# One edge pass over a graph, items of one destination block: destination rows by a one-hot product instead of a gather

## The reference, cut to what matters

```python
h = relu(layernorm(x))
x_i, x_j = h[src], h[dst]                       # 64 features each
out_i = softplus(concat([x_i, edge_attr], -1) @ W).reshape(-1, 4, 64)
out_j = softplus(concat([x_j, edge_attr], -1) @ W).reshape(-1, 4, 64)
alpha = softplus((concat([out_i, out_j], -1) * att).sum(-1))
alpha = softplus(batchnorm(alpha))
alpha = segment_softmax(alpha, src, N)
x = x + segment_sum(out_j * alpha[:, :, None], src, N).mean(1) + bias
```

## Time and profile before

| | us |
|---|---|
| median of 3 runs | 15,799.41 (15,780.74 to 15,803.04) |
| the profiled execution | 15,805.04 |
| its span, first to last instruction | 15,803.4 |
| POOL busy | 10,427.8 (66%) |
| DVE busy | 7,340.1 (46%) |
| PE busy | 7,014.0 (44%) |
| ACT busy | 4,611.6 (29%) |

### The profile page before, as it was taken

One profiled execution on the slowest core, in us unless ns is written; L12 is line 12 of the kernel. 1 busy time (PEld: TensorE's weight loads), 2 busy tenths in 40 slices (PEclk: granted clock), 3 DMA queues, 4 the chain that ended last, 5 costly groups with the idle time before them and its releaser, 6 DMA issues. The chain is left out here.

```text
span 15803.4 us, 144151 instructions
## 1 busy us (share of the span) xinstructions
PE 7014.0 (44%) x27704; PEld 5113.7 (32%) x27704; DVE 7340.1 (46%) x13765; ACT 4611.6 (29%) x8149; POOL 10427.8 (66%) x9774
## 2 busy tenths in 40 slices
PE   2344444444444444420255408953333553333377
PEld 1233333333333333310255402333333333333233
DVE  9566666666666666657377600122222222222301
ACT  5455555555555455521366500000000000000000
POOL 7677777777777777747777770057777447777500
PEclk9777777777766677655566659755555555555578
DMA  0444444444444444490366507521111221111155
GB/s 14 111 129 128 128 129 129 130 129 129 133 129 129 129 129 129 129 78 8 98 183 181 157 5 253 203 62 26 26 26 26 56 77 25 26 26 26 19 191 212
DMA packets 867765, 1601.13 MB, mean 101 GB/s; under 512 B 510485, under 2 KB 518653, under 8 KB 817264
## 3 DMA queue, kind: packets, MB, share of 16 engines
q1 hardware_dynamic: 536176, 1173.07, 24.4%
q0 software_dynamic: 331392, 426.19, 11.6%
HBM read 1091.51 MB, written 505.30 MB: 101 GB/s over the span
## 5 line engine op out<-in xcount | busy, mean ns | idle before, releaser
L1401 POOL DMA_INDIRECT l2s_got<-rel_d,l2s_idx x3232 | 3223.3, 997 | 2141.6 <-POOLq L1398 1244.2
L1427 PE MATMUL l2s_ps<-l2s_got,l2s_oh 128*128 128x65 f32 (+1 forms) x6464 | 1473.3, 421 | 2770.4 <-PEq L1425 2763.5
L1427 PEld LDWEIGHTS l2s_ps<-l2s_got,l2s_oh 128*128 128x128 f32 x6464 | 1409.0, 330 | 2837.5 <-issue 2837.5
L1120 POOL DMA_INDIRECT count_d<-all_list_val,all_list_idx x1568 | 1810.2, 1154 | 503.4 <-issue 463.2
L647 POOL DMA_INDIRECT edge_gath<-h_d,edge_idx_d x1576 | 1682.0, 1067 | 480.3 <-issue 480.3
L643 POOL DMA_INDIRECT edge_gath<-h_d,edge_idx_s x1576 | 1665.0, 1056 | 480.2 <-issue 390.6
L1102 DVE TENSOR_TENSOR net_acc<-net_acc,l2s_ps 128x65 f32 (+1 forms) x3232 | 720.4, 223 | 2705.5 <-DVEq L1449 1813.1
L655 POOL DMA_INDIRECT rows_d<-edge_rows,edge_place x1576 | 1652.7, 1049 | 480.5 <-issue 479.7
L790 DVE SCALAR_TENSOR_TENSOR edge_rows<-edge_z,edge_soft 128x1024 f32<-128x1024 f32 x784 | 952.6, 1215 | 2011.2 <-DVEq L788 2010.9
L723 PE MATMUL edge_z<-edge_w_i,edge_in_i 128*128 128x256 f32 x3140 | 1346.3, 519 | 761.6 <-PEq L752 448.7
L716 PE MATMUL edge_tp<-all_ident,edge_gath 128*128 128x128 f32 x1576 | 428.1, 427 | 1932.5 <-DMA edge_gath<-h_d,edge_idx_d 1649.1
(11 more groups left out here) (342 smaller groups left out, 12493.9 us busy)
## 6 DMA issues: line engine op xcount, KB each, us to landing
at_rows<-rows_d SPq DMA_DIRECT2D x444, 528.0 KB
count_d<-edge_zero SPq DMA_DIRECT2D x196, 1024.0 KB
edge_srow<-in_src SPq DMA_DIRECT2D x197, 512.0 KB, 5.1
edge_lrow<-lo_d SPq DMA_DIRECT2D x197, 512.0 KB, 6.0
l1s_cnt<-count_d SPq DMA_DIRECT2D x49, 1600.0 KB, 6.6
l3s_cnt<-count_d SPq DMA_DIRECT2D x49, 1600.0 KB, 7.0
rel_d<-l2t_out SPq DMA_DIRECT2D x100, 768.0 KB, 3.2
l1s_cnt<-count_d SPq DMA_DIRECT2D x49, 1536.0 KB, 6.7
```

The lines of the kernel that those rows point to most:

```text
L1120: pool.indirect_dma_start(out=cells, out_offset=bass.IndirectOffsetOnAxis(ap=net.list_idx[i][:, k:k + 1], axis=0), in_=net.list_val[i][:, ...
L1401: pool.indirect_dma_start(out=got[r][:, j, 0:cols], out_offset=None, in_=table, in_offset=bass.IndirectOffsetOnAxis(ap=idx[i][:, k:k + 1], ...
L1427: ins = pe.matmul(ps[q][:, j, 0:wide], oh[q][:, j, :], got[r][:, j, 0:wide], start=True, stop=True)
```

## The change

It does these things, all for the edge pass:

- The pass no longer runs over the 1,568 tiles but over the items by destination, 1,616 with padding: 101 trips of two groups. An item has all its valid destinations in one block of 128 nodes. Edges of a tile that belong to the other item go to spare rows.
- The gather of h by dst goes. Per item SP loads the block's 128 rows of h (`nodes`) by a plain DMA, and PE multiplies them with a one-hot of the local destination (`oh_dstT`, from the broadcast row `drow`), which gives the features on partitions at once.
- Edge features are loaded per item, by two DMAs of 64 x 128, since an item's tile is known only at run time (`item`, read into registers).
- The source half is multiplied with W as the stationary side: `z_i` has output features on partitions, 512 edges in a product. Its att dots are 16 products of two columns on PE (`dots`); only the destination half keeps the multiply and reduce on DVE.
- z_i and z_j have one buffer each. The bf16 id rows are half as large; srow is f32.
- The item lists move from `edge_softmax` into a new stage `dst_items` ahead of the edge pass, with a further list of source rows. The 50 counting passes become one comparison of the first destination of each tile (`lead`) with the block bounds.
- `gsrc`, the second list of sources, is gone. The zeros are written in two pieces a group.

```diff
-            def load_group(c0, q):
-                e0 = c0 * P
-                sp.wait_ge(ea_free, 1).then_inc(ea_free, -1)
-                sp.dma_start(in_i[q][D:2 * D, :], a["edge_t"][:, bass.ds(e0, GP)]).then_inc(ea_loaded[q], 16)
-                sp.dma_start(in_j[q][0:D, :], a["edge_t"][:, bass.ds(e0, GP)]).then_inc(ea_loaded[q], 16)
+            def load_group(w0, q):
+                sp.wait_ge(item_listed, 1).then_inc(item_listed, -1)
+                tiles = item_values(nc, sp, item[q][0:1, :, 0], T - 1)
+                blocks = item_values(nc, sp, item[q][0:1, :, 1], NU)
+                sp.wait_ge(feats_free, 1).then_inc(feats_free, -1)
+                for j in range(G):
+                    with Scratch(nc, sp):
+                        sp.dma_start(nodes[q][:, j, :], net.h0_d[bass.ds(blocks[j], P), :]).then_inc(nodes_loaded[q], 16)
+                        for n in TWO:
+                            sp.dma_start(feats[q][D:2 * D, n, j * P:(j + 1) * P],
+                                         edge_tiles[:, bass.ds(tiles[j], 1), :].rearrange("d n e -> d (n e)")
+                                         ).then_inc(feats_loaded[q], 16)
...
                 sp.wait_ge(ids_free, 1).then_inc(ids_free, -1)
+                for row, flat in ((drow, net.loc_d), (lrow, net.low_d), (srow, net.src_d)):
+                    sp.dma_start(row[q][:, :], flat[bass.ds(w0 * P, GP)].partition_broadcast(P)
+                                 ).then_inc(ids_loaded[q], 16)
...
-                    pool.indirect_dma_start(
-                        out=gath[q][:, j, D:2 * D], out_offset=None, in_=net.h0_d,
-                        in_offset=bass.IndirectOffsetOnAxis(ap=idx_d[q][:, j:j + 1], axis=0)
-                    ).then_inc(gathered[q], 16)
...
+                    save(0)
+                    s.wait_ge(zi_ready, 1).then_inc(zi_ready, -1)
+                    softplus_tail(soft_i[:, :], zi, soft_i_ready, 1, 2)
+                    save(3)
+                    s.wait_ge(zj_ready, 1).then_inc(zj_ready, -1)
+                    softplus_tail(soft_j[:, :], zj, soft_j_ready, 4)
+                    save(5)
+                    s.wait_ge(zi_ready, 1).then_inc(zi_ready, -1)
+                    softplus_tail(soft_i[:, :], zi, soft_i_ready, 6, 7)
+                    turn(1 - q)
+                    s.wait_ge(zj_ready, 1).then_inc(zj_ready, -1)
+                    s.sem_inc(feats_free, 1)
+                    softplus_tail(soft_j[:, :], zj, soft_j_ready)
...
+                    outs_i(q, 0)
+                    running(q, 0)
+                    running(q, 1)
+                    outs_j(q, 0)
+                    for j in (2, 3, 4):
+                        running(q, j)
+                    dots(0)
+                    outs_i(q, 1)
+                    running(q, 5)
+                    outs_j(q, 1)
+                    running(q, 6)
+                    running(q, 7)
+                    turn(1 - q, it * (16 * G) + 16 * G * (1 + q), True)
+                    pe.wait_ge(feats_ready, 1).then_inc(feats_ready, -1)
+                    dots(1)
...
+            def dst_hot(q):
+                v.wait_ge(ids_loaded[q], 48).then_inc(ids_loaded[q], -48)
+                v.tensor_scalar(oh_dstT[:, :], drow[q][:, :], net.part[:, 0:1], None,
+                                ALU.is_equal).then_inc(dst_onehot, 1)
...
+                    out_of_i()
+                    dst_hot(1 - q)
+                    ranks(q, 0)
+                    v.wait_ge(dots_ready, 1).then_inc(dots_ready, -1)
+                    v.tensor_copy(dots_i[:, :, :], dots_at[:, :, :]).then_inc(dots_taken, 1)
+                    v.wait_ge(scattered[q], it * (16 * G) + (16 * G if q else 16))
+                    out_of_j(q, 0)
+                    out_of_i()
```

More of the change, by code:

```diff
@@ L308, in _ @@
                     for k in range(some):
-                        ins = pe.transpose(tp[i % 2][:, k, 0:TC], flt[n][:, k0 + k, :], net.ident[0:TC, 0:TC])
+                        ins = pe.transpose(tp[i % 2][:, k, 0:TC], flt[:, k0 + k, :], net.ident[0:TC, 0:TC])
                     ins.then_inc(turned, 1)
+                pe.wait_ge(counted, 1)
+                pe.matmul(tiles[:, :], net.ones[0:TC, :], count[:, :], start=True, stop=True).then_inc(summed, 1)
             @block.vector
@@ L344, in count_dst_blocks_vector @@
[L344 to L352 removed]
+                v.wait_ge(summed, 1)
@@ new lines, in edge_pass @@
+    GROUPS = W // (2 * G)
+    w = e.sb("w", [P, OUTJ])
+    att_i = e.sb("att_i", [P, 2, 2])
+    att_j = e.sb("att_j", [P, OUTJ])
+    before = e.sb("before", [P, P])
+    gath = [e.sb(f"gath{q}", [P, G * D]) for q in TWO]
+    feats = [e.sb(f"feats{q}", [P, 2, GP]) for q in TWO]
+    nodes = [e.sb(f"nodes{q}", [P, G, D]) for q in TWO]
+    srow = [e.sb(f"srow{q}", [P, GP]) for q in TWO]
+    lrow = [e.sb(f"lrow{q}", [P, GP], BF16) for q in TWO]
+    drow = [e.sb(f"drow{q}", [P, GP], BF16) for q in TWO]
@@ new lines, in turn, with outs_i @@
+                    for i in range(HALF):
+                        j = half * HALF + i
+                        ins = pe.matmul(nodes_at[0:D, i, :], nodes[q][:, j, :], oh_dstT[:, j * P:(j + 1) * P],
+                                        start=True, stop=True)
+                    ins.then_inc(nodes_found, 1)
+                pe.wait_ge(feats_loaded[q], 32 * G).then_inc(feats_loaded[q], -32 * G)
+            def outs_i(q, half):
+                for c in TWO:
+                    ins = pe.matmul(z_i[:, c, :], w[:, c * P:(c + 1) * P],
+                                    feats[q][:, 0, half * HP:(half + 1) * HP], start=True, stop=True)
+                ins.then_inc(zi_ready, 1)
@@ new lines, in outs_j, with dots @@
+            def outs_j(q, half):
+                pe.wait_ge(zj_free, 1).then_inc(zj_free, -1)
+                for i in range(HALF):
+                    j = half * HALF + i
+                    ins = pe.matmul(z_j[:, i, :], feats[q][:, 1, j * P:(j + 1) * P], w[:, :], start=True, stop=True)
+                ins.then_inc(zj_ready, 1)
+            def dots(half):
+                pe.wait_ge(zi_free, 1).then_inc(zi_free, -1)
+                for i in range(HALF):
+                    for c in TWO:
+                        ins = pe.matmul(dots_at[:, i, 2 * c:2 * c + 2], out_i[:, c, i * P:(i + 1) * P],
+                                        att_i[:, c, :], start=True, stop=True)
+                ins.then_inc(dots_ready, 1)
@@ L772, in one_hots, with ranks @@
                 v.tensor_scalar(oh_loT[q][:, :], lrow[q][:, :], net.part[:, 0:1], None,
-                                ALU.is_equal).then_inc(onehots, 1)
-                return last
+                                ALU.is_equal).then_inc(src_onehots, 1)
+            def ranks(q, half):
+                for j in range(half * HALF, (half + 1) * HALF):
+                    ins = v.scalar_tensor_tensor(
+                        junk_r[:, j, :], srow[q][:, j * P:(j + 1) * P], src_g[q][:, j:j + 1],
+                        before[:, :], ALU.is_equal, ALU.mult, accum_out=rank[:, j:j + 1])
+                return ins
```

579 lines of the change are left out of this document (303 added, 276 removed).

## The result

The changed kernel takes 17,014.66 us (median of four runs, 16,997.24 to 17,033.58) where the kernel before takes 15,801.23 us (median of four, 15,780.74 to 15,824.59). The ratio is 1.0762, with a 95% interval of 1.0749 to 1.0775: 7.6% slower. The forecast was 17,170 us, in a range of 16,000 to 17,850. The profiled execution took 17,030.77 us, 17,029.2 us of it the span.

The account below looks back on a forecast made before the run. A loop through SP, DVE, PE and ACT was to bound the edge pass: A + B = 38.3 us, 202 groups 7,737 us. 15,805 - 6,452 + 7,737 + 25 + 59 = 17,174, stated as 17,170 us, range 16,000 to 17,850.

Parts of the forecast that it names:

- The bound of before: Edge pass before the change: POOL never idle, 24 indirect DMAs a group at 1.36 us, 32.6 us.
- the loop: Edge pass: one feats_free post leads to the next through SP, DVE, PE and ACT, 38.3 us a group.
- A: From ACT's feats_free post through SP's 24 issues to the landed id rows: 22.8 us, lower bound 19.6.
- B: From the landed id rows through DVE, PE and ACT to the next post: 15.5 us at PE's low clock.
- slower rival: SP: nodes issues cost 1.6 us more, id rows land 1.6 us later; group 41.5 us, 17,820 us; chance 0.13.
- PE keeps its high clock: PE at 2.4 GHz from id rows to post: B 11.1 us, group 33.9, kernel 16,285 us.
- rival of cheaper halves: Either feats issues of 0.33 us (16,530 us) or PE's high clock (16,285 us); groups 31.7 to 36; chance 0.18.
- break-even: Edge-pass group length at which the change neither gains nor loses: 31.5 us.
- fill and drain: Start and end of the edge pass, beside its 202 groups: +25 us.
- The rest: Outside the edge pass: item lists moved ahead of it +110 us, softmax stage 51 us gained, net +59 us.
- The rule beside it: SP's 24 transfers: count costs, not size, 15.8 us; the skill page's estimate gives 19.2 us, near 17,860 us.
- faster rival: Edge pass: loop does not hold; cheap halves 15,640 us, PE at low clock 14,930 or POOL 13,820; chance 0.12.

Follow-up runs that it names:

- rows-first run: Changed kernel with the three id rows asked for on SP ahead of a group's 24 nodes and feats transfers: 14,822.43 us, ratio 0.9368 to the kernel before.
- runs with extra gathers: POOL makes eight more gathers a group that nothing reads: in the changed kernel 17,026.08 us, in that kernel with its id rows first 15,881.80 us.
- all three edits: Changed kernel with id rows first, one transfer for both halves of the features, and the next group's destination one-hot later on DVE: 15,601.72 us.
- single transfer for both halves: Changed kernel with both halves of a tile's edge features written by one transfer that reads its source twice, 16 transfers a group: 16,265.11 us, ratio 1.028.
- later one-hot: Changed kernel with the next group's destination one-hot on DVE after the second out_of_i, not the first: 15,637.84 us, ratio 0.9884 to the kernel before.

## Why the prediction was right, and where its sizes were off

**The bound of before and the loop.** Right. The prediction said that the sum of busy time does not forbid a gain, and that a loop through SP, DVE, PE and ACT takes its place. Each of its five signs is there: DVE idle 13.0 us a group ahead of the one-hot of drow (some 10 were said), 24 issues in 16.33 us (some 16), POOL idle 17.1 us (about 16), groups of 37.46 us (38), and PE waiting 8.2 us for zj_free at the second outs_j. The rows-first run shows it as a cause: the order of the rows on SP alone takes 10.8 us off the group. The runs with extra gathers show the other half, that POOL's relief is worth 5.2 us a group and was worth nothing in this order.

**A, from the post to the rows.** The measured halves meet at SP's first issue, and the forecast's 0.3 us from the post to that issue stood in A. Cut at the same place, the forecast is A 22.5 and B 15.8; measured are 24.99 and 12.36. The issues were right almost exactly: 15.8 + 0.3 = 16.1 against 16.33, at 1.97 us a tile. But a nodes issue took 0.39 and two feats 1.14, a little less and more evenly than I had composed it, with the gaps of the register code the same in sum. The landing was mis-sized. I took 6.4 us from the first row's issue, by the two rows of before; it was 8.66. There are three rows now. The last is asked for 0.97 us after the first, where it was 0.44, and lands 7.3 us later (median), where the last of two took 6.0. The step that failed is "the rows, 1 MB as before in three DMAs": the bytes were the same, the landing was not. It cost 2.3 us in this group. The slower rival had 1.6 us for it. The engines of the DMA are full in the stretch in which the rows land, but they were so before:

```profile
3010.00:3015.00 5.00, 2.53 (x7) 1.12 (x5) 0.00 (x0) 2.17 (x3) 3.78 (x5) 0.81 0.60 119
3015.00:3020.00 5.00, 0.00 (x0) 0.00 (x0) 1.14 (x4) 0.00 (x0) 3.78 (x5) 0.53 1.01 372
```

```profile
3040.00:3045.00 5.00, 3.41 (x11) 2.50 (x10) 0.81 (x5) 2.94 (x6) 3.88 (x4) 0.50 0.96 341
```

The second fence is the kernel before, behind the rows that it asked for at 3036.52. The last three numbers are the clock, the DMA share and GB/s. 372 GB/s over 5 us are 1.86 MB, more than the 1 MB of rows: in both kernels the zeros of the count table, another 1 MB a group, are issued right behind the rows, in the changed one here:

```profile
3011.69 1.32 SPq L750 DMA_DIRECT2D count_d<-edge_zero  x2
```

So a full stretch is not what is new, and it does not explain the longer landing. What is new ahead of the rows are the 24 small transfers, the reason that the slower rival gave. With all three edits nothing stands right ahead of the three rows, and they land as the two did before:

```profile
edge_srow<-src_d SPq DMA_DIRECT2D x203, 512.0 KB, 5.9
```

That fits the rival's reason, but the zeros do not follow the rows at once in that run either, and none takes the small transfers away alone, so the cause of the 2.3 us stays open. The prediction set aside a longer landing with the share of the whole stage, 0.45; that is a mean over 33 us, and says nothing of the microseconds in question.

**B, from the rows to SP's next first issue: 15.8 forecast, 12.36 measured.** I took PE's low clock for all of it, because PE has stood idle. It was low for the first step only: outs_j took 3.59 us, but the transposes took 0.63 and not 1.09, and each half of the nodes 1.09 or 1.06 and not 1.9. The granted clock is 0.53 from 3,015 to 3,020, 0.50 from there to 3,025 and 0.95 from 3,025 to 3,030 (0.50 is 1.2 GHz, 1.00 is 2.4). That is 2.1 of the 3.4 us. Another 0.7 is DVE, whose sum began 1.84 us after the rows, not 2.5: its one-hot of bf16 took 0.75 where the row of f32 had 0.94, the ranks overlap more, and the copy of the dots had been given 0.4. The post is 0.5: SP takes it up 0.19 us before ACT's copy ends in the record (3,031.14 against 3,031.33), not 0.3 us after it. "PE keeps its high clock" was half of the rival of cheaper halves; it was true of two steps in three.

**The two errors, +2.5 and -3.4, nearly cancel.** That the forecast lies within 1% of the result is in this part luck: A's error alone gives 40.8 us a group, B's alone 34.9. The direction and the mechanism do not hang on it, since both are above the 31.5 us of break-even. 37.46 and not 38.3 us a group is 170 us less over 202 groups; fill and drain were 71 us and not 25 (30 us to the first one-hot, 40 from the last). The edge pass is 124 us shorter than forecast: 7,638 against 7,762.

**The rest.** Right: lists +107 us (110 forecast); softmax stage -69 (-51 forecast); so the net was +38 and not +59. 17,174 - 124 - 21 = 17,029, and the profiled execution took 17,031. Most of the distance between forecast and result is the 170 us of the loop.

**The rule beside it.** A transfer of 32 KB took SP 0.39 us (nodes), two of feats 1.12 to 1.14, 24 of them in all 16.33 us. By the Trainium skill, page "DMA: Bandwidth & Descriptors", section Bandwidth, the estimate was 19.2 us for the 24, and the sum 17,860 us. The trace does not bear this out: it has 16.33 us, 0.68 for each transfer. The page's figures are DMA time of transfers issued from GpSimd, and what counted here was SP's issue. The DMA share was 0.17 from 3,031 to 3,041, while SP issued 15 of the 24, and the single transfer for both halves took 3.84 us off SP's time with the bytes as they were.

**The faster rival.** It had 0.12, and "rows land before DVE asks for them" is what the rows-first run makes true. PE was to decide then with 27.2 us, 14,930; it was 26.7 us and 14,822. The total came out close, but not for the rival's reason: its 27.2 us are PE at the low clock without a gap, and in that run PE is busy 82% of the group, 21.9 us, at a mean granted clock of 0.77. So this agreement is luck, and what bounds that kernel is open, as said above.

## What to carry to other kernels

A relief of the busiest engine is worth only what the next loop leaves of it. Follow one "free" post round to the next through every queue, with what stands ahead in each; what is small and wanted first (here 1.5 us of id rows) belongs ahead of what is large and wanted last (16 us of tiles). And move a wait only after looking at what its result releases: the later one-hot freed DVE, but held PE up ahead of the nodes, came with a lower clock on PE, and cost 3.7 us a group in the better order.

A stage's mean of the DMA share says little about one landing. For a landing on the critical path read the window in which it lands, before and after, and what stands in the same queue ahead of it and behind it: here the share was full both times, and the last row took 6.0 and 7.3 us.

## What the runs showed that I had not expected

- SP's issues with register addresses: 0.39 us for 128 rows of 256 bytes, 1.12 to 1.14 for two of 64 pieces of 512 bytes, 0.62 for 64 partitions with two copies of 512 bytes each. One feats issue (0.54 by itself) was dearer than a nodes issue, though each moves 32 KB.
- Granted clock rising inside a short chain: 0.54 in outs_j (3.59 us) behind a wait of 9.68 us, and four transposes in 0.63 us, where they take 1.09 at the low clock, 1.1 us after its end.
- Three broadcast rows of 1 MB in all, with 1 MB of zeros and POOL's DMAs beside them, go through a stretch of full DMA engines (share 1.01, 372 GB/s), and are there 8.7 us after the first is asked for.
- Two chips apart, the same program took 15,801 and 19,065 us, with holes of some us between the instructions of SP, PE, DVE and ACT, while POOL kept its 0.30 us between DMAs. The cause is open.
